# One kernel, one change: the shared expert of a mixture layer computed feature-major, 512 tokens at a time, and the router's sigmoid taken from the silu table

## The reference, cut to what matters

```python
logits = x @ W_gate_router                                   # 4096 x 256 @ 256 x 8
scores = jax.nn.sigmoid(logits)
_, sel = jax.lax.top_k(scores + expert_bias, 2)
top_scores = jnp.take_along_axis(scores, sel, axis=1)
top_scores = top_scores / (top_scores.sum(-1, keepdims=True) + 1e-20)
shared = jax.nn.silu(x @ Wg_s) * (x @ Wu_s) @ Wd_s           # 256 x 192, 256 x 192, 192 x 256
...                                                          # the two chosen experts of each token
out = shared.at[tok].add(routed)
```

## Time and profile before

| what | us |
|---|---|
| median of three executions (916.97 to 922.68) | 918.64 |
| span of the profiled execution | 911.5 |
| PE busy in the span | 831.9 |
| DVE busy | 652.8 |
| ACT busy | 474.6 |
| POOL busy | 379.5 |
| dense half of the mixture, 338.0 to 480.0: PE busy / DVE busy / ACT busy | 118.2 / 108.7 / 97.1 |

### The profile page before, as it was taken

The page is one execution under the profiler, slowest core; times in us unless marked ns, Lnnn a source line. Parts: engine busy times, 40 slices in busy tenths (PEclk is TensorE's granted clock), DMA queues, the critical chain, the costliest instruction groups (busy, mean ns, idle before and its releaser), DMA issues.

```text
span 911.5 us, 16937 instructions
## 1 busy us (share of the span) xinstructions
PE 831.9 (91%) x5115; PEld 744.7 (82%) x5115; DVE 652.8 (72%) x1917; ACT 474.6 (52%) x1006; POOL 379.5 (42%) x427
## 2 busy tenths in 40 slices
PE   6899999999999978889868999999698899988997
PEld 5789998987999877778758999999577788876776
DVE  3666677735567676878784676576768999888986
ACT  2443343434334338777724676466344345449883
POOL 3542200169000014564642445475678886423230
PEclk9799999989999995999998999999899999999999
DMA  9200000000000004242335445334411200000112
GB/s 306 104 1 1 2 1 1 2 1 1 1 1 1 2 22 136 89 140 89 112 112 148 126 129 179 103 112 133 128 47 47 65 29 1 1 1 24 47 47 70
DMA packets 47799, 58.31 MB, mean 64 GB/s; under 512 B 5599, under 2 KB 42848, under 8 KB 47712
## 3 DMA queue, kind: packets, MB, share of 16 engines
q1 hardware_dynamic: 39856, 39.11, 14.5%
q0 software_dynamic: 6480, 16.92, 5.1%
q10 hardware_dynamic: 1376, 1.20, 0.4%
HBM read 34.91 MB, written 23.22 MB: 64 GB/s over the span
## 4 chain that ended last, share of the span: by engine, by line
PE 32%; DVE 15%; issue 6%; ACT 5%; POOL 2%; SPq 1%; DMA 0%; DVEq 0%; ACTq 0%; POOLq 0%
PE bank L80 7%; PE bank L82 7%; PE bank L81 7%; PE bank L1701 2%; PE bank L1709 2%; PE bank L1600 1%; DVE xm L2090 1%; PE bank L1717 1%; PE bank L1721 1%; PE bank L1718 1%; PE bank L1719 1%; PE bank L1720 1%; DVE st L2026 1%; ACT spare L1211 1%; DVE hth L1415 1%
## 5 line engine op out<-in xcount | busy, mean ns | idle before, releaser
L367 ACT CAST pth<-tp 128x512 fp32r<-128x512 f32 (+3 forms) x80 | 41.7, 525 | 128.8 <-PE tp L717 127.4
L1144 POOL DMA_INDIRECT results<-row_tiles,idu x71 | 70.0, 986 | 89.0 <-ACT row_tiles L1293 75.0
L1128 POOL DMA_INDIRECT region<-row_tiles,posu x64 | 66.3, 1035 | 59.8 <-DVE posu L1399 42.7
L547 DVE TENSOR_TENSOR ptl<-tp,pth 128x512 fp32r<-128x512 f32 (+3 forms) x80 | 48.2, 607 | 54.7 <-ACT pth L367 54.6
L80 PE MATMUL cx<-vh,pth 128*128 128x256 f32 x272 | 80.6, 296 | 1.4 <-DVE ptl L547 1.2
L82 PE MATMUL cx<-vh,ptl 128*128 128x256 f32 x272 | 76.8, 282 | 0.0
L81 PE MATMUL cx<-vl,pth 128*128 128x256 f32 x272 | 76.8, 282 | 0.0
L80 PE MATMUL sc<-hh,ph 128*128 128x512 f32 (+3 forms) x160 | 61.0, 381 | 0.3
L82 PE MATMUL sc<-hh,pl 128*128 128x512 f32 (+3 forms) x160 | 58.3, 364 | 0.0
L81 PE MATMUL sc<-hl,ph 128*128 128x512 f32 (+3 forms) x160 | 58.1, 363 | 0.0
L358 ACT ACTIVATE prob<-sc,nmx 128x512 f32<-128x512 f32 (+3 forms) x80 | 49.4, 628 | 14.0 <-DVE nmx L520 14.0
(11 more groups left out here) (430 smaller groups left out, 2787.0 us busy)
## 6 DMA issues: line engine op xcount, KB each, us to landing
row_tiles<-region SPq DMA_DIRECT2D x71, 130.0 KB, 2.3
pairs_a<-results SPq DMA_DIRECT2D x10, 512.0 KB
x<-in_x SPq DMA_DIRECT2D x8, 512.0 KB, 10.7
out<-x SPq DMA_DIRECT2D x8, 512.0 KB, 2.9
pairs_b<-results SPq DMA_DIRECT2D x6, 512.0 KB, 4.9
early<-in_wmod SPq DMA_DIRECT2D x2, 768.0 KB, 4.6
early<-in_wmod SPq DMA_DIRECT2D x1, 1536.0 KB, 8.3
spare<-in_wg SPq DMA_DIRECT2D x8, 192.0 KB, 2.7
```

Of the source, the lines that this page charges most:

```text
L367: a_.copy(pth[:, m % 2, 0:w], tp[:, m % 2, 0:w]).then_inc(s["pt_hi"], 1)
L547: vec.tensor_tensor(ptl[:, m % 2, 0:w], tp[:, m % 2, 0:w], pth[:, m % 2, 0:w], ALU.subtract).then_inc(s["pt_lo"], 1)
L1128: g_.indirect_dma_start(region, bass.IndirectOffsetOnAxis(ap=posu[:, c, t:t + 1], axis=0), hb[:, G % HB, j], None).then_inc(scattered[G % ...
L1144: g_.indirect_dma_start(results, bass.IndirectOffsetOnAxis(ap=idu[:, j % 8:j % 8 + 1], axis=0), y[:, j % YR, 0:D], None, bounds_check=KS * ...
```

## The change

The shared expert is now feature-major over all 512 tokens of a group. The host joins its two weights, with the columns in another order, into `wgu_s`: gate features 128 to 191 and value features 128 to 191 make one block of 128, then come the gates 0 to 127, then the values 0 to 127. `dense_up(G, m)` holds a block's weights still and streams 512 tokens past them: six matmuls of 128x512 for each of three blocks, into three PSUM banks (`up3`). The result has its features on the partitions, as `dense_down` needs them, so nothing is turned. `gate_b` and `product_b` handle the mixed block (64 partitions), `gate_a` and `product_a` the large one; `hi_b`, `hi_a`, `low_b` and `low_a` split the products into `fh` and `fl`. `dense_down(G, i)`, i = 0 and 1, makes two tiles each (ten matmuls of 128x256) and stands one group later than `dense_up`. `add(G, i)` adds 512 columns at once.

The router's sigmoid: `logit_of` on DVE takes the logits out of PSUM (with 1e-20 in the place of an exact zero) and makes their reciprocal; ACT takes silu of the logits, x times sigmoid(x), and DVE multiplies by the reciprocal. So ACT uses one table in the stage. PE's first `turn_h`, which overwrites the bank of the logits, waits for `logit_set` in place of the sigmoid. The buffers `fh`, `fl` and `act2` take room from ones that are free in this stage; the sparse half loses only the offsets of its counters (N1).

The diff, cut to its core:

```diff
@@ ScalarE
             def sigmoid(G):
-                act.wait_ge(s["logits"], G + 1)
-                need(act, s["route"], G)
-                a_.activation(sig[:].rearrange("p t e -> p (t e)"), bk[:, 0:GT * E], ACT.Sigmoid).then_inc(s["sig_done"], 1)
+
+                act.wait_ge(s["logit_set"], G + 1)
+                a_.activation(sig[:], logit[:], ACT.Silu).then_inc(s["sig_done"], 1)
...
+            def gate_b(G):
+                act.wait_ge(g["up_ready"], G * 3 + 1)
+                need(act, g["lo"], G * 2 - 1)
+                if G == 0:
+                    act.wait_ge(s["w_lo"], 2)
+                a_.activation(act2[F - P:P, 1], up3[0:F - P, 0], ACT.Silu).then_inc(g["silu_done"], 1)
+
+            def gate_a(G):
+                act.wait_ge(g["up_ready"], G * 3 + 2)
+                need(act, g["lo"], G * 2)
+                a_.activation(act2[:, 0], up3[:, 1], ACT.Silu).then_inc(g["silu_done"], 1)
+
+            def hi_b(G):
+                act.wait_ge(g["product"], G * 2 + 1)
+                need(act, g["down_ready"], G * 2)
+                a_.copy(fh[F - P:P, 1], act2[F - P:P, 1]).then_inc(g["hi"], 1)
+                a_.copy(fh[0:F - P, 1], act2[F - P:P, 1]).then_inc(g["hi"], 1)
+
+            def hi_a(G):
+                act.wait_ge(g["product"], G * 2 + 2)
+                need(act, g["down_ready"], G * 2)
+                a_.copy(fh[:, 0], act2[:, 0]).then_inc(g["hi"], 1)
...
             sigmoid(0)
+            h_back(0, 0)
+            h_back(0, 1)
+            h_of(1)
             up_weights(1, 0)
             down_weights(1, 0)
-            h_back(0, 0)
-            h_back(0, 1)
             for G in range(1, GROUPS + 1):
-                n = (G - 1) * GT
+                gate_b(G - 1)
                 if G < GROUPS:
-                    h_of(G)
-                silu(n)
-                if G < GROUPS:
+                    h_hi(G)
                     sigmoid(G)
-                    h_hi(G)
-                if n:
-                    ht_hi(n - 1)
-                silu(n + 1)
-                ht_hi(n)
+                hi_b(G - 1)
+                if G + 1 < GROUPS:
+                    z_of(G + 1)
+                gate_a(G - 1)
                 if G < GROUPS:
                     h_back(G, 0)
+                    up_weights(G + 1, G)
+                    h_back(G, 1)
+                hi_a(G - 1)
                 if G + 1 < GROUPS:
-                    z_of(G + 1)
-                silu(n + 2)
-                ht_hi(n + 1)
+                    h_of(G + 1)
                 if G < GROUPS:
-                    h_back(G, 1)
-                silu(n + 3)
-                ht_hi(n + 2)
-                if G < GROUPS:
-                    up_weights(G + 1, G)
                     down_weights(G + 1, G)
-            ht_hi(N1 - 1)
@@ VectorE
+            def logit_of(G):
+                v.wait_ge(s["logits"], G + 1)
+                flat = lambda a: a.rearrange("p t e -> p (t e)")
+                c_.link(vec.tensor_scalar(flat(logit[:]), bk[:, 0:GT * E], 0.0, 1e-20, ALU.is_equal, ALU.mult))
+                vec.tensor_tensor(flat(logit[:]), flat(logit[:]), bk[:, 0:GT * E], ALU.add).then_inc(s["logit_set"], 1)
+                v.wait_ge(s["logit_set"], G + 1)
+                c_.link(vec.reciprocal(sel[:], logit[:]))
 
             def choose(G):
                 q = slice(G * GT, (G + 1) * GT)
                 v.wait_ge(s["sig_done"], G + 1)
+                c_.link(vec.tensor_tensor(sig[:], sig[:], sel[:], ALU.mult))
...
+            def product_a(G):
+                v.wait_ge(g["silu_done"], G * 2 + 2)
+                v.wait_ge(g["up_ready"], G * 3 + 3)
+                vec.tensor_tensor(act2[:, 0], act2[:, 0], up3[:, 2], ALU.mult).then_inc(g["product"], 1)
...
+            for G in range(1, GROUPS):
+                product_b(G - 1)
+                logit_of(G)
+                h_lo(G)
+                if G > 1:
+                    add(G - 2, 0)
+                choose(G)
+                low_b(G - 1)
+                if G > 1:
+                    add(G - 2, 1)
+                weigh(G)
+                low_up_weights(G + 1, G)
+                product_a(G - 1)
+                rank_of(G)
+                low_a(G - 1)
+                low_down_weights(G + 1, G)
@@ TensorE
+            def dense_up(G, m):
+                if m == 0:
+                    pe.wait_ge(s["lo_h"], (G + 1) * KC)
+                    if G == 0:
+                        pe.wait_ge(s["w_lo"], 1)
+                need(pe, g["product"], G * 2 - 1 if m == 0 else G * 2)
+                q = slice(m * P, (m + 1) * P)
+                for e in range(KC):
+                    last = three(nc.tensor, up3[:, m], gsh[:, e, q], gsl[:, e, q], hh[G % 2][:, e], hl[G % 2][:, e], e == 0, e == KC - 1)
+                last.then_inc(g["up_ready"], 1)
+
+            def dense_down(G, i):
+                pe.wait_ge(g["lo"], (G + 1) * 2)
+                pe.wait_ge(g["hi"], (G + 1) * 3)
+                need(pe, g["x_added"], G * 2 + i)
+                mm, wh, wl = nc.tensor.matmul, dsh[:, G // GPB], dsl[:, G // GPB]
+                for j in (2 * i, 2 * i + 1):
+                    q, out = slice(j * P, (j + 1) * P), dp[:, (j % 2) * D:(j % 2 + 1) * D]
+                    mm(out, fh[:, 0, q], wh[:, 0], start=True, stop=False)
+                    mm(out, fh[:, 0, q], wl[:, 0], start=False, stop=False)
+                    mm(out, fl[:, q], wh[:, 0], start=False, stop=False)
+                    mm(out, fh[:, 1, q], wh[:, 1], start=False, stop=False)
+                    last = mm(out, fh[:, 1, q], wl[:, 1], start=False, stop=True)
+                last.then_inc(g["down_ready"], 1)
...
+            turn_h(0, 0)
             turn_z(1)
-            turn_h(0, 0)
+            turn_h(0, 1)
             pe.wait_ge(s["consts"], 1)
             count(0)
-            turn_h(0, 1)
...
+            for G in range(1, GROUPS):
+                dense_up(G - 1, 0)
+                logits(G)
+                if G > 1:
+                    dense_down(G - 2, 0)
+                dense_up(G - 1, 1)
+                if G > 1:
+                    dense_down(G - 2, 1)
+                turn_h(G, 0)
+                dense_up(G - 1, 2)
+                turn_h(G, 1)
+                if G + 1 < GROUPS:
+                    turn_z(G + 1)
+                count(G)
```

## The result

The changed kernel takes **1.0064 times** the kernel before, with a 95% interval of 1.0039 to 1.0089 (20 executions of each). On 918.64 us that is 924.5 us (922.2 to 926.8): 0.6% slower, within the 1% of the forecast and inside its own range of 913 to 926, but above the 919 that the sum gave. The medians of all 20 are 917.84 and 926.55. The ratios here leave out executions at a lower granted clock, among them three of the changed kernel's 20 and the profiled one of the second experiment, of which only the order of its rows is used.

The account below looks back on a forecast made before the run. A loop over three engines, ScalarE, TensorE and VectorE, was taken as the bound. Terms at full clock gave -9.5 us and clock falls +10.2, net +0.7 on 918.64: 919 us, range 908 to 934.

Parts of the forecast that it names:

- The loop's links: Steps from one `h_of` to the next across three engines, summed to 14.7 us against 15.33, 0.63 less per group.
- `hi_b`'s wait: On ScalarE, `hi_b` would idle 3 us in each group until `dense_down` released it, holding up the queue behind it.
- The clock: TensorE's clock would fall behind the logits in every group, costing 1.7 us in each of six loops, +10.2 us.
- rival 1: No clock fall on the loop's path: the full-clock sum stands, 909 us, `h_of` spacing 14.7; chance 0.22.
- rival 2: A second thin stretch, TensorE waiting 2.2 us before the second `turn_h`, keeps the loop's clock low: 933 us; chance 0.28.
- Table loads: In the expert stage's dense half, 15 of 16 go; costed at nothing, being covered by ScalarE's wait for TensorE.
- the detour of the logits: `logit_of` and the added product, some 0.2 us each, would lie under `dense_down` and `dense_up`, 4.2 us long.
- The start: The stage's piece up to the second `h_of` would shrink by 1.9 us, bounds 0 and -3.
- the first loop: From the second `h_of`, without `dense_down` but at the lower clock: 14.0 us against 15.34, -1.3.
- a sign against its sum: A loop path leading through the choice on VectorE, or a spacing under 14 us, would make the sum wrong.
- The end of the last loop: Without `z_of` and with the ranks ahead of `hi_a`: 13.1 us against 16.2, -3.1 at full clock.
- the two chains behind the ranks: SyncE's clearing of the region and the chain to the last addition: about equally long, so the shift carries over.

Follow-up runs that it names:

- the second experiment: The changed kernel with the sigmoid from its own table again, without the reciprocal and the product by it; 1.0233 times the kernel before.
- e3: The changed kernel with the next group's normalisation ahead of `hi_b` in ScalarE's list instead of behind it; 0.9983 times the kernel before.
- e6: The changed kernel with the normalisation ahead of `hi_b` and, on VectorE, the large product ahead of `weigh` and the weights' low part; 0.9779 times the kernel before.
- e1: The kernel before with only the router's half of the change (silu of the logits times their reciprocal); 1.0040 times the kernel before.
- e8: The changed kernel with the sigmoid's own table, normalisation ahead of `hi_b`, and a one-column silu putting both table loads into `hi_b`'s wait; 0.9993 times the kernel before.
- e4: The changed kernel with the end of the dense half reordered: group 6's `dense_down` and its additions come earlier; 1.0032 times the kernel before.
- e7: e6 plus the reordered tail of e4 and the last half of `dense_down` in a bank of its own; 0.9787 times the kernel before.
- e5: The changed kernel with 18 extra matmuls of 128x256 per loop, their result unread, ahead of the second `turn_h`; 1.0034 times the kernel before.
- e9: The changed kernel with only VectorE's large product moved ahead of `weigh` and the weights' low part; 1.0027 times the kernel before.

## Why the prediction was right, and where not

- **The loop's links.** Summed to 14.7 us at full clock; the loop of 424.93 measures 15.05. From the router's first matmul to `hi_b` 6.37 (426.42 to 432.79) for 6.02, and `hi_b` 1.29 for 1.06: its casts of 64 partitions lie 0.65 apart, longer than the 0.53 of the cast of 128 that priced them. Right in kind.
- **`hi_b`'s wait**: 3 us forecast, 3.70 found; TensorE's wait ahead of `turn_h` 2.2 and 2.63. e3 and e6 show that it cost.
- **The clock.** Forecast: a fall in every loop behind the logits, 1.7 each, 8.5 in the five steady loops. Found: the five take 79.57 us (376.02 to 455.59), 4.3 over five of 15.05, a mean spacing of 15.9 between the 14.7 of rival 1 and the forecast's 16.4. The place was wrong: in one steady loop of five a fall stood behind the logits (379 to 383), and three falls stood behind the second wait (389.5 to 396.5, 406.5, 437), so the second thin stretch of rival 2 is real. The price of a fall is 0.5 to 2.1 us here, since part of each lies beside other work. Against the earlier trace rows, 76.66 for the same five, the loops lost 2.9 us, where the sum had 5.3.
- **Table loads** hidden: right (e1, e8). That the detour of the logits was hidden too holds in the change, where `hi_b` waits behind the sigmoid; alone it costs 0.45 us a group (e1), and I had not weighed the halves apart.
- **The start**: -1.9 forecast for the piece up to the second `h_of`, -1.2 found (11.87 to 10.68); the first loop -1.3 forecast, +0.15 found (15.49 against 15.34). There the router starts 3.46 us behind `h_of` (360.53 to 363.99) where 1.5 were counted, since a `dense_up` at the low clock stands ahead of it, and behind the logits the chain of waits runs through VectorE's choice, which the prediction had named as a sign against its sum.
- **The end of the last loop**: -3.1 and +1.7 for a fall forecast; 13.8 against 16.2, -2.5 found (455.59 to 469.35), with no fall behind its logits.
- **The step that failed** in the sum is the sentence that the two chains behind the ranks "are about equally long, so the shift carries over". They are not: 22.5 us against 17.2, **+5.3**. SyncE's chain did keep its length (14.2 for 14.7), but the other grew from 15.4 to 20.7. The prediction gave no sum for it. On the trace `dense_down` of group 6 is split around the last two `dense_up`, the last low part stands behind VectorE's counting, and the clock is low from 471.5 to 475 and again from 481.7. By the spacings of the matmuls (0.43 for 0.23 in seven, 0.21 for 0.12 in twenty) the low clock is some 3.3 of the 5.3, an estimate. e4 and e7 shorten the tail by 1.8 (469.80 to 490.46) and 5.5 (445.53 to 462.50).

So the sum of -1.2, +0.2, +2.9, -2.5 and +5.3 is +4.7 where +0.7 stood. The errors have opposite signs and partly cancel: the steady loops came out 2.4 and the last loop 1.1 better than forecast, since the clock was priced too high; the start came out 2.2 and the tail 5.3 worse. That the time fell into the range is in part luck: the range was wide for the clock's sake, and the tail wasn't in it.

Which of TensorE's waits has to go for the clock to hold? The profiles answer for this loop: both. e3 and e5 shortened the one ahead of `turn_h` to about 0.5 and kept 1.24 and 0.85 us ahead of the router: falls, behind the router's burst. e9 closed the one ahead of the router and kept 2.61 ahead of `turn_h`: falls, behind `turn_h`. e6 and e7 closed the one ahead of the router and shortened the other to 0.54: none in the steady loops. What stays open is how short is short enough (in the kernel before, falls followed a wait of 0.24), and why some waits of 2.63 bring a fall and others, in the same kernel, don't.

## What to carry to other kernels

Fewer instructions and fewer table loads bought nothing here: the loop is a ring over three engines, and what counts is what stands *behind* a wait on an in-order queue. Put independent work (the next group's normalisation) ahead of a wait, not behind it, and the operand that the ring waits for (the product) ahead of work that nobody waits for. When a change leaves holes of two or three microseconds on TensorE, price the loop at both clocks: here the same work took 12.4 us without them (e6) and 14.3 to 19.8 with one in each loop (e9, steady loops). And count both chains of a stage's end before calling them equal.

## What the runs showed of the hardware that I had not expected

- With the wait ahead of the router closed and the other at 0.54 us, the loop kept the clock up. Of the 2.7 to 4.8 us a loop that e6 gains on the change's steady loops (15.05 to 17.17, now 12.35), 2.7 are the shorter path, by the loop of 15.05 that no fall lengthened; the rest, up to 2.1, is the clock, which stayed at 1.00.
- The fixed start of the program takes 59 or 65.5 us from one execution to the next, and the granted clock differs with it (0.67 to 0.77 from 26 to 32 us in the five profiles with the early start, 0.50 in the six others): a difference larger than the effect under study. Which of the two brings the other isn't shown. A stage is compared from its own start.
- An instruction over 64 partitions is no cheaper than one over 128: `hi_b`'s casts take 0.62 each, as `hi_a`'s does, and VectorE's 64x512 product 0.69 as the 128x512 one (0.68).
